# Turning the softmax probabilities by DMA block exchange and VectorE in a fused attention block

## What is computed

```python
x = x + _L0_xattn_ref(_layernorm(x, axis=-1), ctx_4096)
x = x + _L0_attn_ref(_layernorm(x, axis=-1), L0_attn_Wq, L0_attn_bq, L0_attn_Wk, L0_attn_bk, L0_attn_Wv, L0_attn_bv)
x = x + _L0_ffn_ref(_layernorm(x, axis=-1), L0_ffn_W_base, L0_ffn_b_base, L0_ffn_W_gate, L0_ffn_A, L0_ffn_B)
```

```python
def _L0_xattn_ref(query, key):
    a = jnp.einsum('bqd,bkd->bqk', query, key)
    e = jax.nn.softmax(a, axis=-1)
    c = jnp.einsum('bqk,bkd->bqd', e, key)
    return c
```

## Time and profile before

| | |
|---|---|
| time, median of 3 runs | 2468.36 us (2467.91 to 2469.70) |
| time of the profiled execution | 2470.24 us |
| its span | 2468.4 us |
| granted TensorE clock, mean | 0.997 |
| TensorE (PE) busy | 2439.6 us, 99% |
| VectorE (DVE) busy | 1967.1 us, 80% |
| ScalarE (ACT) busy | 1100.0 us, 45% |
| GpSimd (POOL) busy | 1412.6 us, 57% |
| DMA moved | 519.80 MB, mean 211 GB/s |

### The profile page before, as it was taken

One profiled execution on the slowest core, in us unless ns is written; L12 is line 12 of the kernel. 1 busy time (PEld: TensorE's weight loads), 2 busy tenths in 40 slices (PEclk: granted clock), 3 DMA queues, 4 the chain that ended last, 5 costly groups with the idle time before them and its releaser, 6 DMA issues. The chain is left out here.

```text
span 2468.4 us, 36112 instructions
## 1 busy us (share of the span) xinstructions
PE 2439.6 (99%) x11446; PEld 2013.2 (82%) x11446; DVE 1967.1 (80%) x2706; ACT 1100.0 (45%) x1577; POOL 1412.6 (57%) x1052
## 2 busy tenths in 40 slices
PE   6999999999999999999999999999999999999999
PEld 5888888888888888888888888888888888877777
DVE  7888788887888887888888888888888888874466
ACT  4444444444444444444444444444444444433553
POOL 2766666666766565564655566565556566561541
PEclk9999999999999999999999999999999999999999
DMA  9988878888788978988888888988898888789643
GB/s 224 260 227 209 226 207 230 223 201 230 206 231 218 226 204 220 216 215 214 218 219 213 212 220 205 229 209 208 220 224 206 215 219 218 189 201 203 178 128 100
DMA packets 434167, 519.80 MB, mean 211 GB/s; under 512 B 66886, under 2 KB 308550, under 8 KB 431688
## 3 DMA queue, kind: packets, MB, share of 16 engines
q1 hardware_dynamic: 424136, 477.23, 79.0%
q0 software_dynamic: 9984, 41.95, 5.2%
HBM read 488.71 MB, written 30.41 MB: 210 GB/s over the span
## 5 line engine op out<-in xcount | busy, mean ns | idle before, releaser
L621 POOL TENSOR_TENSOR nat_lo<-raw,nat_hi 128x512 fp32r<-128x512 f32 x784 | 1171.7, 1525 | 863.5 <-ACT nat_hi L781 830.7
L1082 DVE TENSOR_TENSOR ch_lo<-tr,ch_hi 128x512 fp32r<-128x512 f32 x784 | 762.7, 973 | 296.2 <-ACT ch_hi L770 292.5
L770 ACT CAST ch_hi<-tr 128x512 fp32r<-128x512 f32 x784 | 481.1, 621 | 797.1 <-PE ps L1491 781.1
L1489 PE MATMUL ps<-ch_hi,xt_hi 128*128 128x512 f32 x1696 | 669.8, 395 | 4.8 <-DVE ch_lo L1082 4.8
L1491 PE MATMUL ps<-ch_hi,xt_lo 128*128 128x512 f32 x1696 | 662.5, 391 | 0.0
L1490 PE MATMUL ps<-ch_lo,xt_hi 128*128 128x512 f32 x1696 | 662.1, 390 | 0.0
L1489 PE MATMUL ps<-nat_hi,pt_hi 128*128 128x512 f32 x1568 | 610.6, 389 | 0.0
L1491 PE MATMUL ps<-nat_hi,pt_lo 128*128 128x512 f32 x1568 | 610.6, 389 | 0.0
L1490 PE MATMUL ps<-nat_lo,pt_hi 128*128 128x512 f32 x1568 | 610.4, 389 | 0.0
L1078 DVE STREAM_TRANSPOSE tr<-quart 128x512 f32<-128x512 f32 x784 | 547.6, 699 | 2.6 <-DMA quart<-in_ctx_dram 2.6
L781 ACT CAST nat_hi<-raw 128x2048 fp32r<-128x2048 f32 x196 | 374.5, 1911 | 208.0 <-PE ps L1491 188.3
(11 more groups left out here) (202 smaller groups left out, 1377.1 us busy)
## 6 DMA issues: line engine op xcount, KB each, us to landing
quart<-in_ctx_dram SPq DMA_DIRECT2D x392, 512.0 KB, 8.4
raw<-in_ctx_dram SPq DMA_DIRECT2D x196, 1024.0 KB, 8.6
wq_in<-in_L_attn_Wq_dram POOLq DMA_DIRECT2D x16, 1024.0 KB, 6.4
win<-in_L_ffn_W_base_dram SPq DMA_DIRECT2D x64, 256.0 KB, 6.8
tr<-wt_dram POOLq DMA_DIRECT2D x64, 256.0 KB, 3.6
wt_dram<-stage SPq DMA_DIRECT2D x32, 256.0 KB, 5.6
wt_dram<-stage_b SPq DMA_DIRECT2D x32, 256.0 KB, 10.3
wq_dram<-wq_out POOLq DMA_DIRECT2D x16, 256.0 KB, 2.3
```

What stands on the lines that cost most here:

```text
L621: last = pool.tensor_tensor(nat_lo[:, j, t], raw[:, j % 2, t], nat_hi[:, j, t].bitcast(F32), ALU.subtract)
L770: act.copy(ch_hi[:, c % RING_CH, :], tr[:, c % RING_TR, :]).then_inc(chunk_hi, 1)
L1082: dve.tensor_tensor(ch_lo[:, c % RING_CH, :], tr[:, c % RING_TR, :], ch_hi[:, c % RING_CH, :].bitcast(F32), ALU.subtract).then_inc(chunk_s ...
L1489: pe.matmul(out_, a_hi, b_hi, start=start, stop=False)
```

## The change

For the turns 2 to 48 (`turn.by_dma`, 47 of them) TensorE no longer transposes the probabilities. ScalarE writes `probs` with its columns in another order. SP copies it, in four DMAs for each q, to a new buffer `quads` (in the place of `b_nat`): each takes 128 columns of all 128 partitions and lays them on 32 partitions, four rows of 512 bytes to a partition. VectorE then turns `quads` in 32x32 blocks back into `probs` (`turn_probs`), one instruction for each q, and `pt_hi` and `pt_lo` are made from `probs` in SBUF, not from `ps`. Turn 1 and the virtual end turn stay as they were. Around it:

- SP waits for the softmax of the next turn at the end of each `next_block` and issues the eight DMAs there. `W_base`'s rows are loaded earlier, between the last two `raw` loads of step 1 and not after them; the store of the fifth turned piece comes before the second half of `quart`, and VectorE turns that piece at c = 10, not 14. `stage2` has a place of its own.
- TensorE's pieces 0 and 1 come after the chunks 6 and 8, not 5 and 7. VectorE adds pieces 0 and 1 at c = 10 and 12, not 9 and 11. Late additions come ahead of the group work, and the transpose of chunk c + 3 comes after both. ScalarE's row piece 0 comes at c = 12, not 11.
- All eight DMAs of `load_expert` are issued in the last turn, after `quads` is free.

```diff
-        stage2 = put(at_probs + 12 * KIB, "stage2", [P, 4 * P])
+        stage2 = sb("stage2", [P, 4 * P])
+        quads = put(at_b, "quads", [P, TT, QR, P])
+                self.by_dma = not (self.first or self.second or self.over)
-        PIECE_AFTER = {5: 0, 7: 1, 9: 2, 11: 3, 13: 4, 15: 5}
+        PIECE_AFTER = {6: 0, 8: 1, 9: 2, 11: 3, 13: 4, 15: 5}
+            def move_next_probs(turn, q):
+
+                sp.wait_ge(probs_ready, turn.times(TT, q + 1))
+                for b in range(QR):
+                    sp.dma_start(quads[b * SQ:(b + 1) * SQ, q], probs[:, q, b * P:(b + 1) * P]).then_inc(probs_moved[q], 16)
@@ next_block
+                if step == 1:
+                    store_turned(m, 4)
                 next_quarters(turn, 1, quarter(turn.times(KB, KB), 1))
                 if step == 0:
                     store_turned(m, 1)
                 for j in range(2):
+                    if j == 1 and step == 1:
+                        sp.wait_ge(wt_stored[4], m * 16 + 16)
                     sp.wait_ge(nat_ready[j], turn.times(1, 1))
                     load_rows(j + 2, ctx_rows(turn.times(KB), j + 2))
                     if j == 0 and step == 1:
-                        store_turned(m, 4)
+                        sp.wait_ge(wt_stored[3], m * 16 + 16)
+                        load_win(m + 1)
                 if step == 0:
                     store_turned(m, 2)
-                if step == 1:
-                    for k in (3, 4):
-                        sp.wait_ge(wt_stored[k], m * 16 + 16)
-                    load_win(m + 1)
+                for q in range(TT):
+                    move_next_probs(turn, q)
...
             next_block(REST[0], LAST_M)
-            for e in range(EXPERTS // 2):
-                load_expert(e)
...
             sp.dma_start(x_nat[:], x_dram).then_inc(x_again, 16)
-            for e in range(EXPERTS // 2, EXPERTS):
+            sp.wait_ge(lo_drained, G_PT + TT * (NB - 1))
+            for e in range(EXPERTS):
                 load_expert(e)
@@ ScalarE, softmax and probs_group
-                act.activation(probs[:, q, :], ps[:, SCORE_BANK + TT * new + q, :], ACT.Exp,
+                to, of = probs[:, q, :], ps[:, SCORE_BANK + TT * new + q, :]
+                if turn.by_dma:
+                    to = to.rearrange("p (b t j) -> p t b j", b=QR, t=KT)
+                    of = of.rearrange("p (t b j) -> p t b j", b=QR, t=KT)
+                act.activation(to, of, ACT.Exp,
...
+                if turn.by_dma:
+                    act.wait_ge(out_ready, turn.times(8, 6 + q + 1 - 16))
+                    hi_group(turn.times(TT, G_PT + q - TT), q, pt_hi[:, q], probs[:, q].rearrange("p (t m) -> p t m", t=KT))
...
-            ROWS = {11: 0, 15: 1}
+            ROWS = {12: 0, 15: 1}
@@ VectorE
+            def turn_probs(turn, q):
+
+                dve.wait_ge(probs_moved[q], turn.times(16 * QR, -16 * QR))
+                dve.transpose(probs[:, q].rearrange("p (t i a) -> p t a i", t=KT, a=QR),
+                              quads[:, q].rearrange("p a (t j) -> p t a j", t=KT)).then_inc(group_done, 1)
...
-            ADD_AFTER = {9: 0, 11: 1, 13: 2, 15: 3, 17: 4}
+            ADD_AFTER = {10: 0, 12: 1, 13: 2, 15: 3, 17: 4}
...
                     lo_chunk(turn.times(DC, c), c)
+                    if c in ADD_LATE_AFTER and lagging:
+                        add_late_piece(turn, ADD_LATE_AFTER[c])
+                    if c == (7 if turn.second else 5) and not turn.first:
+                        if turn.by_dma:
+                            for q in range(TT):
+                                turn_probs(turn, q)
+                        for q in range(TT):
+                            probs_group(turn, q)
                     n = c + AHEAD
                     if n < DC or not turn.last:
                         transpose_chunk(turn.times(DC, n), n, turn.times(16 * QR, 16 * QR * (n // DC)))
...
@@ TensorE
+                elif turn.by_dma and v < TT:
+                    pe.wait_ge(lo_drained, turn.times(TT, G_PT - 1 + v))
...
-                    if c == (3 if turn.second else 1) and not turn.first:
+                    if c == 3 and turn.second:
                         for q in range(TT):
                             probs_group(turn, q)
...
-TURN_AFTER = {(0, 8): 0, (0, 12): 1, (0, 16): 2, (1, 4): 3, (1, 14): 4}
+TURN_AFTER = {(0, 8): 0, (0, 12): 1, (0, 16): 2, (1, 4): 3, (1, 10): 4}
```

More of the change, by code:

```diff
@@ L311, in perceiver_block @@
         probs_ready = sem("probs_ready")
+        probs_moved = [sem(f"probs_moved{q}") for q in range(TT)]
         alpha_ready = sem("alpha_ready")
@@ L793, in probs_group @@
             def probs_group(turn, q):
-                hi_group(turn.times(TT, G_PT + q - TT), q, pt_hi[:, q], bank4(q))
+                if turn.by_dma:
+                    act.wait_ge(out_ready, turn.times(8, 6 + q + 1 - 16))
+                    hi_group(turn.times(TT, G_PT + q - TT), q, pt_hi[:, q], probs[:, q].rearrange("p (t m) -> p t m", t=KT))
+                else:
+                    hi_group(turn.times(TT, G_PT + q - TT), q, pt_hi[:, q], bank4(q))
             def row_piece(turn, j):
@@ L1131, in add_late_piece @@
                                          ALU.mult, ALU.add).then_inc(acc_updated, 1)
+            def turn_probs(turn, q):
+                dve.wait_ge(probs_moved[q], turn.times(16 * QR, -16 * QR))
+                dve.transpose(probs[:, q].rearrange("p (t i a) -> p t a i", t=KT, a=QR),
+                              quads[:, q].rearrange("p a (t j) -> p t a j", t=KT)).then_inc(group_done, 1)
             def probs_group(turn, q):
-                lo_group(turn.times(TT, G_PT + q - TT), pt_lo[:, q], bank4(q), pt_hi[:, q])
-            ADD_AFTER = {9: 0, 11: 1, 13: 2, 15: 3, 17: 4}
+                src = probs[:, q].rearrange("p (t m) -> p t m", t=KT) if turn.by_dma else bank4(q)
+                lo_group(turn.times(TT, G_PT + q - TT), pt_lo[:, q], src, pt_hi[:, q])
+            ADD_AFTER = {10: 0, 12: 1, 13: 2, 15: 3, 17: 4}
             ADD_LATE_AFTER = {3: 5, 5: 6, 7: 7}
@@ L1165, in iteration @@
                         transpose_chunk(turn.times(DC, n), n, turn.times(16 * QR, 16 * QR * (n // DC)))
-                    if c == (7 if turn.second else 5) and not turn.first:
-                        for q in range(TT):
-                            probs_group(turn, q)
-                    if c in ADD_LATE_AFTER and lagging:
-                        add_late_piece(turn, ADD_LATE_AFTER[c])
                     if c == 7 and not turn.first:
```

## The result

The changed kernel takes 2445.44 us (median of 4 runs, 2443.54 to 2448.39), the kernel before 2468.69 on the same chip (4 runs, 2467.91 to 2469.70). The ratio is 0.9909, 95% interval 0.9897 to 0.9921: 23 us faster. The forecast was 2431.0 with a range of 2424 to 2453. The sign and the range hold; the forecast is 14.4 us too low, and the narrower range of its likeliest case, 2425 to 2439, doesn't hold the time. The profiled execution took 2443.54. Lines after the change are numbered anew: the matmuls are L1518 to L1520, `turn_probs` L1155, the softmax L802, `ch_lo` L1101, `pt_lo` L1042, SP's copies L495, the experts' loads L534.

What follows compares the result with a forecast made beforehand. TensorE's instruction stream was taken to bound the turns. From 2470.24 us, 43.2 came off for transposes, 5.1 on for the last turn, 1.9 off for median against profiled execution, 1 on for the start: 2431 us, range 2424 to 2453.

Steps and rivals of the forecast that it cites:

- likeliest case: Whole kernel: 2431 us, own range 2425 to 2439, with tail 0 to 11.6 us; chance 0.52.
- first term: TensorE's eight transposes, 0.92 us a turn, fall away in 47 turns: 43.2 us gained.
- the forecast's sum: Whole kernel: TensorE's gain of 43.2 us, less a last-turn loss of 5.1 and 1 for the start: 2431 us.
- The reordered edits: `ROWS`, `ADD_AFTER` and transposes behind the additions, in the turns: cost nothing, covered by the 1.4 us slack.
- for small waits at the start, where the DMA share is highest, I add 1: Start of the kernel: small waits cost 1 us, bringing 2430.2 to 2431.
- The price of `turn_probs`: VectorE's turning of one tile in each turn: 0.66 us taken, bounds 0.66 and twice it.
- the slack of 1.4 us: VectorE has chunk 6 ready 1.4 us before TensorE wants it; 0.1 with the strided output at its upper bound.
- The tail's number: Last turn: extra expert loads delay `raw`, so TensorE waits; 5.1 us lost, bounds nothing and 11.6.
- the late copies: Rival: copies late where `win` stands in front, 1 us in 16 turns or 0.35 in all 47: 2447; chance 0.20.
- The slower rival: Every turn: softmax to `pt_lo` exceeds 10 us, copies land after 8.4 us, 1.5 us late; 2501 us, chance 0.13.
- VectorE's wait for `quads` under 1 us in nearly all turns: Sign in the new profile that the forecast is right: VectorE waits under 1 us for the copies.
- TensorE doesn't wait for `ch_lo`: Sign in the new profile that the forecast is right: no TensorE waits for `ch_lo`; waits each turn mean wrong.

Runs made afterwards that it cites:

- r5: The changed kernel with neither copies nor VectorE's turnings, the probabilities used unturned; a one-element instruction stands for each turning: 2431.5 us, ratio 0.9853.
- r12: The changed kernel with turn 2 on TensorE's transposes and the experts' loads behind the last `raw` loads, without copies and turnings: 2426.03 us, ratio 0.9827.
- r2: The changed kernel with turn 2 alone back on TensorE's transposes: 2441.64 us, ratio 0.9889.
- r6: The changed kernel with VectorE's turnings writing a dense output, so the queries of a tile come out permuted: 2443.39 us, ratio 0.9900.
- r10: The changed kernel with turn 2 on TensorE and late experts' loads, without copies; the turnings read other data: 2429.62 us, ratio 0.9840.
- r1: The changed kernel once more, unaltered, as the base for its sibling runs: 2447.13 us, ratio 0.9917 to the kernel before.
- r3: The changed kernel with the experts' loads behind the last `raw` loads, after `b_base`'s load in SP's order: 2442.83 us, ratio 0.9902.
- r4: The changed kernel with `load_win` left at the end of SP's order for the turn, in front of the copies: 2462.84 us, ratio 0.9979.

## Why the prediction was nearly right

**The bound and the first term held.** TensorE's stream set the pace, and eight transposes were worth 0.92 us a turn: undisturbed turns fell from 44.4 to 43.5. r5 put the forecast's sum (2431) on the chip as 2431.5, and r12, with the tail mended and turn 2 on TensorE, has 42.8 us less than the kernel before, where 46 turns of 0.92 make 42.3. The reordered edits, which the prediction costed at nothing, are in both, and turns 3 to 48 show no loss by them.

The page VectorE: DVE Perf Modes of the Trainium skill, section Rules for kernel authors, with its rule for TensorE, would have kept the old way. The rows decide otherwise: even with all its losses the way round is 23 us faster.

**The step that failed is "for small waits at the start, where the DMA share is highest, I add 1".** The start cost 8.5 us in turn 2. The step looked at the DMA share; what counted was SP's order, in which the copies stand behind a `raw` load, and that waited 8.7 us for GpSimd. They went out 4.7 us after the softmax began instead of 0.8. The prediction had checked that SP is free in the turn at 1023, and in no other turn. And it priced a wait at its own length: the low clock with this one added 3.0 us. r2 takes both away. Some 2 of the 8.5 us are no cost of the copies or turnings (r5).

**The price of `turn_probs` was too low.** Taken was 0.66, bounds 0.66 and 1.3. It took 1.08, and r6 shows that the output's stride is the cause. With SP's issues at 5.09 / 8 = 0.64 where 0.48 was taken, the second turned tile ended 1.3 us later than forecast, counted from the softmax. That is the slack of 1.4 us, as the prediction said of the upper bound. Outside turn 2, the turns with W_base missed 2.4 us, turn 47 1.5 and turns 3 to 16 2.4. The price of `turn_probs` alone doesn't explain that: with full turnings and no copies, r10 loses nothing in turns 17 to 47, and r6's dense output didn't make the time shown shorter. With the slack used up, a copy that lands late gets through. In turns 3 to 16 single turns are up to 1.3 us longer, in r1 turns 3 and 4 and in r2 turns 7 and 16; what picks them stays open. VectorE's busy share came out as forecast: 77.13 of 87.05 us, 89% for 88%.

**The tail's number held:** 5.1 forecast, 4.4 by the trace, 4.3 by r3's time and 3.4 by its trace. Its way was partly another one, so the fit is in part luck. The prediction had one wait for `nat_lo` of 4.2. TensorE waited 1.4 for it, 1.8 for `pt_lo`, since ScalarE cast the late `raw` first and `pt_hi` behind it, and 1.7 for a `nat_lo` of the next phase.

**The rivals.** The number of the late copies, 2447, is nearer to the result than the forecast is, but not by its cause: it had 16 us from all turns or from those with W_base, and there the profiled execution missed 2.4. (That part varies: by the same count it is 6.8 in r1, 8.2 in r2 and 2.1 in r3.) The largest loss was a late copy too, but in turn 2 and behind `raw`. r4 shows what the rival is worth: with `win` directly in front of the copies the kernel is 15.7 us slower, at 2463. The prediction costed that edit as "1.9 us at least" of delay; SP's part was 0.1 us in the turn shown, the rest is the transfer's. The slower rival (a landing after 8.4 us in every turn) fell: 2.9 in the median, 7.5 at most. "VectorE's wait for `quads` under 1 us in nearly all turns" held (17 waits, 7.5 us); "TensorE doesn't wait for `ch_lo`" didn't hold in 8 places.

**The ledger.** This is for the profiled execution. Forecast 2431. Turn 2 +8.5, less the 1 us set aside; turns 3 to 47 +6.3; tail -0.7; the start up to the second softmax -2.3, which is chance (the first softmax came between 50.9 and 53.2 in kernels whose work up to there is the same). That is 2441.8. The forecast had taken off 1.9 because the kernel before's median was below its profiled execution; with them back it is 2443.7, and the execution took 2443.54. The median of the changed kernel is 1.9 above that, within its spread.

## What to carry to other kernels

Taking a short burst off the bounding engine pays its whole pitch per turn, if the way round is done before the slack ends; price that way in the first and the last turns by themselves, since their queues are in another state than those in the middle. When a short transfer joins a queue, what stands in front of it decides, in the queue and in the issuing engine's order with all that it waits for: the place of one 1 MB load was worth 15.7 of the 21.5 us that r1 gained. A row that merges two issues can hide a wait between them; ask for the issuer's waits. A wait of the bounding engine can cost more than its length, through the clock.

## What the runs showed of the hardware

- A VectorE transpose of 128x512 f32 whose output has a stride of 16 bytes takes 1084 ns, a dense one 699.
- After 5.28 us without a matmul, TensorE's granted clock was 0.50 for some 6 us of dense matmuls, which cost 3.0 us more. After the wait of 1.76 us at 2158.14 it stayed at 1.00. In r2's tail it was 0.53 between 2160 and 2165 after a wait of 3.3 us.
- `pt_lo` took 0.67 us when GpSimd was idle (1025.77) and 1.6 when GpSimd worked beside it (104 to 107 us); that GpSimd is the cause was not tested by itself.
- Copies of 64 KB in packets of 512 bytes from SBUF to SBUF land 2.9 us after issue in the median, and up to 8.5 behind larger loads (r4).
